# Moving one small matmul block of a triangular solve to the end of its turn, in a fused decoder layer

## The reference

```python
x = x + _L0_attn_ref(_layernorm(x), ...)           # delta rule: inv, u, w, scan over chunks, gates, Wo
x = x + _L0_xattn_ref(_layernorm(x), ctx_1024, ctx_1024, mask, ...)
x = x + _L0_ffn_ref(_layernorm(x), ...)

# in the delta rule
inv = -(kb @ jnp.swapaxes(k, -1, -2)) * strict_lower
for i in range(1, chunk):
    inv = inv.at[..., i, :].add(jnp.einsum('...j,...jk->...k', inv[..., i, :], inv))
inv = inv + jnp.eye(chunk)
u = inv @ v
w = inv @ kb
...
# in the attention
scores = jnp.einsum('bhqd,bhkd->bhqk', Q, K) / np.sqrt(D_HEAD)
attn = jax.nn.softmax(jnp.where(mask == 0, -jnp.inf, scores), axis=-1)
out = jnp.einsum('bhqk,bhkd->bhqd', attn, V)
```

## Time and profile before

| | |
|---|---|
| median of 3 runs | 1323.07 us (1318.98 to 1323.56) |
| the profiled execution | 1323.56 us |
| its span, first to last instruction | 1321.8 us |
| PE busy in the span | 1119.9 us, 85% |
| DVE, ACT, POOL busy | 958.0 us, 898.0 us, 653.0 us |
| mean granted TensorE clock | 0.895 of full |

### The profile page before, as it was taken

One profiled execution on the slowest core, in us unless ns is written; L12 is line 12 of the kernel. 1 busy time (PEld: TensorE's weight loads), 2 busy tenths in 40 slices (PEclk: granted clock), 3 DMA queues, 4 the chain that ended last, 5 costly groups with the idle time before them and its releaser, 6 DMA issues. The chain is left out here.

```text
span 1321.8 us, 28637 instructions
## 1 busy us (share of the span) xinstructions
PE 1119.9 (85%) x9251; PEld 820.2 (62%) x9251; DVE 958.0 (72%) x2132; ACT 898.0 (68%) x1743; POOL 653.0 (49%) x2200
## 2 busy tenths in 40 slices
PE   5998988783678799999999999999999888885756
PEld 4776766683566566766776776676677655443225
DVE  5999998698355657777877877777787566633985
ACT  5999998221344558787878878877887665453867
POOL 4777775563225544465465466547546543111007
PEclk9999998555557869999999999999999988897989
DMA  2443433893412434343433434343442342203106
GB/s 80 159 176 144 177 136 144 185 234 107 137 57 85 110 80 127 95 124 109 133 110 106 146 105 138 106 129 105 111 144 82 96 127 57 65 33 140 44 1 223
DMA packets 141779, 154.17 MB, mean 117 GB/s; under 512 B 48040, under 2 KB 106560, under 8 KB 141632
## 3 DMA queue, kind: packets, MB, share of 16 engines
q1 hardware_dynamic: 141632, 152.35, 38.4%
HBM read 93.32 MB, written 58.72 MB: 115 GB/s over the span
## 5 line engine op out<-in xcount | busy, mean ns | idle before, releaser
L2120 DVE TENSOR_REDUCE x_maxima<-x_psA 128x2 f32<-128x512 f32 x248 | 170.3, 687 | 96.2 <-PE x_psA L1448 93.7
L1704 ACT ACTIVATE x_PT<-x_psB 128x512 f32<-128x512 f32 x240 | 143.0, 596 | 56.5 <-PE x_psB L1472 52.1
L1711 ACT ACTIVATE x_psA<-x_mask_q 128x512 f32<-128x512 bf16 x239 | 142.4, 596 | 51.8 <-DVE x_maxima L2120 48.7
L297 DVE SCALAR_TENSOR_TENSOR a_conv<-a_ps_proj,taps,a_conv 128x253 f32<-128x253 f32 (+2 forms) x288 | 115.0, 471 | 8.4 <-ACT a_conv L364 8.4
L1448 PE MATMUL x_psA<-x_Ks,x_Qs 96*128 96x256 bf16 x496 | 99.5, 283 | 15.2 <-ACT x_psA L1711 14.7
L1469 PE MATMUL x_psB<-x_mask_k,x_ident_bf 128*128 128x512 bf16 x240 | 94.3, 393 | 13.0 <-ACT x_PT L1704 10.8
L533 PE MATMUL a_ps_proj<-a_hT,wqkv 128*128 128x256 f32 x384 | 93.2, 392 | 7.1 <-DVE a_conv L297 4.2
L1472 PE MATMUL x_psB<-x_Qs,x_Ks 98*128 98x256 bf16 x480 | 94.1, 277 | 0.0
L533 PEld LDWEIGHTS a_ps_proj<-a_hT,wqkv 128*128 128x128 f32 x384 | 71.5, 194 | 19.4 <-issue 6.6
L1864 POOL TENSOR_SCALAR x_parts_q<-x_rest 128x512 bf16<-128x512 f32 x16 | 23.9, 1494 | 116.3 <-DVE x_rest L2096 116.3
L1486 PE MATMUL x_psO<-x_PT,x_V 128*32 128x256 f32 x1024 | 72.0, 401 | 1.0 <-ACT x_PT L1704 1.0
(11 more groups left out here) (390 smaller groups left out, 3352.8 us busy)
## 6 DMA issues: line engine op xcount, KB each, us to landing
scratch_keypack<-a_keypack SPq DMA_DIRECT2D x16, 768.0 KB, 3.3
c_keypack<-scratch_keypack SPq DMA_DIRECT2D x16, 768.0 KB, 4.7
x_Ks<-scratch_k_parts SPq DMA_DIRECT2D x192, 64.0 KB, 2.2
b_matrix<-in_long_padded SPq DMA_DIRECT2D x16, 512.0 KB, 7.4
scratch_k_parts<-x_parts_k SPq DMA_DIRECT2D x32, 192.0 KB, 2.4
scratch_q_parts<-x_parts_q SPq DMA_DIRECT2D x32, 192.0 KB, 2.3
x_Qs<-scratch_q_parts SPq DMA_DIRECT2D x32, 192.0 KB, 3.0
a_x_in<-in_x SPq DMA_DIRECT2D x16, 256.0 KB, 2.7
```

Source lines behind the costliest of these rows:

```text
L297: nc.vector.scalar_tensor_tensor(acc, ps_proj[PROJ_BANK[p]][:, c, 0:L - j], taps[:, p, c, TAPS - 1 - j:TAPS - j], acc, ALU.mult, ALU.add). ...
L1704: nc.scalar.activation(PT[:, k % (2 * GROUP)], bank_B(b, k)[0], ACT.Exp, scale=XD ** -0.5).then_inc(pexp_ready, 1)
L1711: nc.scalar.activation(psA[:].rearrange("p t q -> p (t q)"), mask_q[:, k % 2].rearrange("p s k -> p (s k)"), ACT.Copy).then_inc(mask_writt ...
L2120: nc.vector.tensor_reduce(maxima[:, t, 2 * pair:2 * pair + 2], bank_A(b, k)[0], AX.X, ALU.max).then_inc(maxed, 1)
```

## The change

The operations `p1` and `w5` are moved in the table. Before, they stood behind `mA15` and ahead of `maxT`. Now `p1` stands behind `vc`, ahead of `sA0`, and `w5` is the last entry. The waits on `ps_join` follow: `maxT` of row b waits for the masked gram of row b + 4 (`attn_ready`, which the DVE signals) where it waited for `w5`; `p1` of row b waits for `sh2` of row b - 4, and where no such row exists (b below 4) for `attn_ready` of its own row as before; `p2` loses its wait on `sh2`.

```diff
@@ C_ORDER
            (5, "sB15"), (5, "eB15"), (2, "og1"), (2, "gelu2"), (4, "sA15"), (5, "pv3"), (0, "att1"), (3, "st_qp"), (3, "ld_Q0"),
-           (4, "mA15"), (0, "p1"), (0, "w5"), (4, "maxT"), (4, "sh1"), (1, "stats"), (1, "st16"), (3, "ld_Q1"), (4, "sh2"), (4, "ld_S"), (3, "kA0"),
-           (5, "OT1"), (3, "Q0st"), (0, "sums3a"), (3, "vproj"), (3, "vc"), (3, "sA0"), (3, "mA0")]
+           (4, "mA15"), (4, "maxT"), (4, "sh1"), (1, "stats"), (1, "st16"), (3, "ld_Q1"), (4, "sh2"), (4, "ld_S"), (3, "kA0"),
+           (5, "OT1"), (3, "Q0st"), (0, "sums3a"), (3, "vproj"), (3, "vc"), (0, "p1"), (3, "sA0"), (3, "mA0"), (0, "w5")]
@@ block.tensor
                 elif op == "p1":
                     pe.wait_ge(nAT_ready, 2 * b + 2)
                     pe.wait_ge(T_ready, b + 1)
-                    pe.wait_ge(attn_ready, 2 * b + 2)
+                    after(pe, b, (shift_ready, -4, 1, 1), (attn_ready, 0, 2, 2))
@@
                 elif op == "p2":
                     pe.wait_ge(W32_ready, b + 1)
-                    after(pe, b, (shift_ready, -4, 1, 1))
@@
                 elif op == "maxT":
                     pe.wait_ge(maxed, HEAD_STEPS * (b + 1))
-                    after(pe, b, (W32_ready, 4, 1, 1), (h3T_ready, -3, 1, 1))
+                    after(pe, b, (attn_ready, 4, 2, 2), (h3T_ready, -3, 1, 1))
```

## The result

| | before | changed |
|---|---|---|
| median | 1321.03 us (1317.31 to 1323.56, 4 runs) | 1338.3 us (1335.5 to 1341.93, 4 runs) |
| ratio, with all seven runs of the changed kernel | | 1.0138, 95% interval 1.011 to 1.0166 |

I had forecast 1323.3 and 1316 to 1330. The kernel became 17 us slower. The profiled execution of the changed kernel is longer than any of those seven: its span is 1347.3 us, theirs are 1333.7 to 1340.1.

The account below looks back on a forecast made before the run. PE was taken to set the pace, idle 2.3 to 2.6 us a turn. Eleven turns +0.4, turn 4 -0.4 and turn 3 0 sum to 0.0; between profile and median that put the time at 1323.3 us, range 1316 to 1330.

Parts of the forecast that it names:

- The wait that goes and the wait that comes: On PE, waits of 0.95 before `maxT` and 0.22 before `ctxT` go; one of about 1.3 us before `p1` comes.
- The distance of `sh2` from `oT8`: Sign to check: `sh2` on DVE would still start 7.25 us behind `oT8` on PE, as before.
- DVE's wait for POOL: Sign to check: DVE's wait before `st16` for the end of POOL's `stats` would stay at 2.8 us.
- The sum for a turn: PE's time up to `ctxT`: +0.04 us per turn, +0.4 in the eleven turns where DVE waited for POOL.
- Turn 4: The one `maxT` wait without a `st16` wait ahead of `sh2`: `ctxT` at 491.45 instead of 491.89, -0.4 us.
- Rival D: A later `sA0` delays the scores' chain by 0.30 us in eleven turns, 3.3 in all: 1326.6 us; chance 0.06.
- rival C: PE's idle piece before `p1` lets the clock fall, 1.7 us in each of eleven turns: 1342 us; chance 0.07.
- Rival B: `sh2` is early, so `p1` follows `vproj` without a wait: 14.7 us faster, 1308.6 us; chance 0.10 with softer forms.

Follow-up runs that it names:

- e3: Changed kernel with five unread 128x512 matmuls filling PE's idle time ahead of `p1` in turns 5 to 15: 1329.44 us against 1321.23, ratio 1.0047.
- e7: Kernel before with `vproj` between `p1` and `maxT`, `sA0` and `mA0` ahead of `sh2`, `sums3a` last: 1317.95 us against 1317.52, ratio 1.0002.
- e9: The changed kernel as it is, timed and traced a second time beside the kernel before: 1337.72 us against 1317.52, ratio 1.016.
- e4: Kernel before with one more 32x256 copy on ACT ahead of `w5`, lengthening PE's wait before `maxT`: 1326.66 us against 1323.01, ratio 1.0032.
- e1: Changed kernel with `sh2` taken ahead of `stats` and `st16` in the table: 1321.62 us against 1321.23, ratio 0.9999.
- e6: Changed kernel with two unread 128x512 matmuls ahead of `p1` in turns 5 to 15: 1333.85 us against 1323.01, ratio 1.0072.
- e5: Changed kernel with `sh2` ahead of `st16` and `st16` moved behind `mA0`: 1329.13 us against 1323.01, ratio 1.0036.
- e8: Changed kernel with five unread 128x512 matmuls between `tT` and `p2` in rows 5 to 15: 1341.19 us against 1317.52, ratio 1.0182.

## Why the prediction was wrong, point by point

- **The wait that goes and the wait that comes: right.** 0.95 and 0.22 went, and 1.28 came eleven times (forecast 1.2 to 1.4), put down to `sh2`. The match is a little lucky: I had counted 1.32 from where `vproj` gives way, and by that count it is 1.45 (586.74 to 588.19), since the way from `sh2` to `p1` took 0.15 and not 0.06. The distance of `sh2` from `oT8` stayed, DVE's wait for POOL stayed at 2.8.
- **The sum for a turn: mis-sized.** Forecast +0.04, bounds +0.02 to +0.16; measured +0.34 at full clock (e3, and the undisturbed turns of the changed kernel). I added up to `ctxT` and stopped there, where 9.06 against 8.97 was inside the bounds. The next step, `ctxT` to `tT`, I took as unchanged; it grew by 0.23. It isn't the removed wait that laid this open, as e7 has no wait there and 0.46; it comes with `p1` ahead of the step, as in turn 2 of the kernel before (0.77), of which I had used the step ahead of it only the earlier trace rows. The 0.34 in eleven turns make 3.8 us.
- **Turn 4: right in mechanism.** Its step from `mA15` to `ctxT` shrank as forecast: 4.01 against 4.42 (forecast 3.98), and `ctxT` stands 3.27 behind `maxT`, as the 3.2 of the forecast.
- **Rival D didn't come.** PE's wait for the mask of the scores, 490 to 1030 us, was 0.9 us, once, before as after (e9, e3).
- **The clock, rival C: this is the step that failed.** I gave it 0.07 with the words that PE's total idle time in a turn hardly changes. By the waits that was nearly true (1.17 in two pieces, then 1.28 in one) and beside the point. e4 has more idle time and no fall; e1 has `p1` at the new place without the idle time, and one fall; the two together have 7 to 9 of 11. The reading that fits all of them is that it counts what stands around the idle time; that is argued from these runs, no single one isolates it. In the old order 0.95 us of idle were followed by `maxT` and 1.7 us of `vproj`. In the new one 1.3 us are followed by `p1`, `sA0`, `og2`, `ctxT`, `tT` and `p2`, all of them short or narrow. The eleven falls of 1.7 us that I had priced are 7 to 9, each turn with one 1.2 to 1.7 or 2.9 to 3.1 us longer than the same turn of e3. The eleven turns of e3, without a fall, take 514.6 us, so the falls are 12.9 of the 16.6 us in e9 (527.5 - 514.6) and 22.0 of the 25.7 in the trace of the changed kernel.
- **The Trainium skill's warning** ("TensorE: Matmul & The Clock Gate", section "A second HAM failure mode: psum-queue depth-cycling") that short, frequent idle times can make the clock swing was the one I set aside by the nine steady turns. The trace after agrees with it, with 9 falls in 11 turns in which no wait of PE is longer than 1.3 us. The steady turns only showed that this order didn't swing, not how near it was.
- **Rival B's price was wrong too:** with `sh2` early (e1) the time is 1321.6, not 1308.6, as DVE, ACT and POOL give the gain back.

What stays open: which quantity the clock follows, and why some turns fall and others with the same instructions don't (e6, each second one). With the idle piece alone (e4) or the order alone (e1) there was no fall or one; with both there were 7 to 9, and 5 and 6 with a shorter piece of 0.9 (e6, e5); filling the piece (e3) took all of them away, and work added beside it (e8) most. That is no rule yet.

## What to carry to other kernels

When an edit moves short matmuls next to a wait, price the clock: list what PE does for some microseconds on either side of each idle piece, before and after, since the sum of idle time over a turn says nothing about it. Follow the sum past the last wait that changes, to the matmuls behind the block that was moved, as they can start later than they did. And before you count a removed wait as gain, look at what else in the same queue, on the other engines, was waiting for the same slow chain.

## What I had not expected of the hardware

- PE stood 1.38 us in one piece in each of eleven turns without a fall of the clock (e4), and with 0.85 at another place the clock fell in 5 of 11 turns (e6).
- The step from `ctxT` to `tT` took 0.46 or 0.47 with `p1` at its old place, with a wait of 0.22 ahead of it (before) and without one (e7), and 0.70 with the 32x32 matmuls of `p1` shortly ahead of it (e3, e9).
- The way from the end of a DVE instruction to the first matmul it releases was 0.15 for `p1` (582.46 to 582.61) and 0.06 for `oT8` in the earlier trace rows.
